# Input gates of a GRU quad in three chunks of 512 columns instead of four of 384

## The reference

```python
def cell(h, x):                       # 64 times, one after the other
    gi = x @ W_ih + b_ih              # [32, 512] @ [512, 1536]
    gh = h @ W_hh + b_hh
    r = sigmoid(i_r + h_r);  z = sigmoid(i_z + h_z)
    n = tanh(i_n + r * h_n)
    return (1.0 - z) * n + z * h
x = x + all_h                         # x: [32, 64, 512]
# blocks of 8 steps are summed, keys = blocks @ Wk.T with an RMS norm, softmax of keys . q
attended = einsum('bn,bnh->bh', attn, blocks)
y = x + attended @ Wo.T
x = x + layernorm(y) * ln_gamma + ln_beta
```

## Time and profile before

| what | us |
|---|---|
| median of 3 runs | 372.4 (371.16 to 372.96) |
| profiled execution, its own time | 371.04 |
| span from its first to its last instruction | 369.2 |
| TensorE busy | 361.8 (98%) |
| weight loads on record | 211.9 (57%) |
| VectorE busy | 264.3 (72%) |
| ScalarE busy | 167.5 (45%) |
| GpSimd busy | 11.9 (3%) |
| recurrent matmuls L628, 1920 records | 167.3 |
| input-gate matmuls L597, 720 records | 247.1 |

### The profile page before, as it was taken

How to read it: one execution, slowest core, us unless ns; L and a number is a source line. 1 busy time by engine, 2 the same in 40 slices (tenths; PEclk the granted TensorE clock), 3 DMA queues, 4 the chain that set the end, 5 groups by cost and what they waited for, 6 DMA issues and landing times.

```text
span 369.2 us, 9842 instructions
## 1 busy us (share of the span) xinstructions
PE 361.8 (98%) x3276; PEld 211.9 (57%) x3276; DVE 264.3 (72%) x1144; ACT 167.5 (45%) x525; POOL 11.9 (3%) x46
## 2 busy tenths in 40 slices
PE   8999999999999999999999999999999999999995
PEld 4456666555666555666555666555666655534762
DVE  2936767687676768776768767676868676888886
ACT  4834336262625343452626262434435255857430
POOL 6000000000000000000000000000000000000000
PEclk9999999999999999999999999999999999999999
DMA  7954635413232322324141323232232413110138
GB/s 308 419 157 102 193 93 167 110 36 100 74 99 71 99 71 58 91 64 107 44 105 42 99 71 99 71 99 70 51 99 57 113 38 77 52 30 28 33 136 320
DMA packets 27637, 38.37 MB, mean 104 GB/s; under 512 B 3033, under 2 KB 19033, under 8 KB 27617
## 3 DMA queue, kind: packets, MB, share of 16 engines
q1 hardware_dynamic: 27600, 38.09, 35.6%
q10 hardware_dynamic: 16, 0.02, 0.0%
HBM read 17.91 MB, written 4.19 MB: 60 GB/s over the span
## 4 chain that ended last, share of the span: by engine, by line
PE 90%; DVE 4%; issue 3%; DMA 1%; ACT 1%; DVEq 0%; POOLq 0%; SPq 0%; POOL 0%; ACTq 0%
PE gates_ps L628 43%; PE gi_ps L597 37%; PE gi_ps L610 1%; DVE gcx L1205 1%; PE first_ps L678 1%; PE fourth_ps L628 1%; PE third_ps L628 1%; PE keys_ps L628 1%; PE first_ps L628 1%; PE fourth_ps L678 1%; PE third_ps L678 1%; PE keys_ps L678 1%; DMA h_tok<-hist 1%; PE fourth_ps L666 1%; PE gates_ps L660 0%
## 5 line engine op out<-in xcount | busy, mean ns | idle before, releaser
L628 PE MATMUL gates_ps<-w_hh,turned 128*32 128x384 f32 x1920 | 167.3, 489 | 0.4 <-DVE turned L854 0.3
L628 PEld LDWEIGHTS gates_ps<-w_hh,turned 128*32 128x32 f32 x1920 | 56.4, 109 | 84.7 <-issue 55.5
L597 PE MATMUL gi_ps<-w_ih_hi,xt_hi 128*128 128x384 f32 x240 | 86.7, 363 | 0.0
L478 ACT ACTIVATE rz<-gates_ps 128x256 f32<-128x256 f32 x59 | 22.7, 385 | 128.5 <-PE gates_ps L628 128.5
L597 PE MATMUL gi_ps<-w_ih_hi,xt_lo 128*128 128x384 f32 x240 | 80.7, 338 | 0.0
L597 PE MATMUL gi_ps<-w_ih_lo,xt_hi 128*128 128x384 f32 x240 | 79.7, 334 | 0.0
L916 DVE TENSOR_TENSOR rz<-gates_ps,rz 128x128 f32<-128x128 f32 x59 | 17.2, 292 | 75.6 <-ACT rz L478 75.5
L597 PEld LDWEIGHTS gi_ps<-w_ih_hi,xt_hi 128*128 128x128 f32 x240 | 44.9, 187 | 37.5 <-issue 37.5
L597 PEld LDWEIGHTS gi_ps<-w_ih_lo,xt_hi 128*128 128x128 f32 x240 | 45.1, 188 | 0.0
L597 PEld LDWEIGHTS gi_ps<-w_ih_hi,xt_lo 128*128 128x128 f32 x240 | 44.9, 187 | 0.0
L854 DVE STREAM_TRANSPOSE turned<-hist 128x32 f32<-128x32 f32 x189 | 36.1, 216 | 2.1
(11 more groups left out here) (232 smaller groups left out, 297.1 us busy)
## 6 DMA issues: line engine op xcount, KB each, us to landing
gi<-gi_tok SPq DMA_DIRECT2D x60, 192.0 KB, 3.4
x1t<-in_x_t_dram SPq DMA_DIRECT2D x16, 256.0 KB, 3.2
gcx<-in_x_tok_dram SPq DMA_DIRECT2D x16, 256.0 KB, 3.2
h_tok<-hist SPq DMA_DIRECT2D x64, 64.0 KB, 2.2
out_dram<-gcx SPq DMA_DIRECT2D x16, 256.0 KB, 2.1
gcx<-in_w_ih_dram SPq DMA_DIRECT2D x4, 768.0 KB, 6.7
w_hh<-in_w_hh_dram SPq DMA_DIRECT2D x4, 768.0 KB, 9.0
wo_t<-in_wo_t_dram SPq DMA_DIRECT2D x1, 1024.0 KB, 5.7
```

The source lines that it names most:

```text
L478: act.activation(rz[:], gates_bank(t)[:, P:3 * P], ACT.Sigmoid).then_inc(rz_ready, 1)
L597: mm = pe.matmul(gi_ps[tok][:, 0:G3], a[:, k, :], w[:, k, gi_cols(j)], start=(m == 0), stop=(m == 3 * NJ - 1))
L628: mm = pe.matmul(gates_bank(t)[j * B:(j + 1) * B, P:], before[:, k * B:(k + 1) * B], chunk(w_hh, k, j), start=False, stop=(k == NJ - 1), s ...
```

## The change

The input gates of a quad are cut otherwise: 3 chunks of 512 columns (a whole PSUM bank) instead of 4 of 384. Chunk 0 is r and z of quarters 0 and 1, chunk 1 r and z of quarters 2 and 3, chunk 2 n of all four. The 36 matmuls are dealt out by nines: `gi_part` number 0 in the step tt = 3 of the quad two before it, parts 1 to 3 at tt = 0, 1, 2. So chunk 0 ends 3 matmuls into part 1, chunk 1 6 matmuls into part 2, chunk 2 at the end of part 3. keep_gi and move_gi run at tt = 0, 1, 2 and not at tt = 3. A chunk of r and z is moved by two DMAs (128 KB each, 1 KB pieces), that of n by four (64 KB each, 512 B pieces), so eight moves per quad, counted by one semaphore for each kind of chunk. ScalarE waits for the r and z moves alone before a quad's first seed, and VectorE waits for the n moves before n_pre in a quad's first step. Three bias quarters are copied before the scan and the fourth in step 0. gi_tok grows by 1 KB per partition, and small tiles of the end move to free columns of b_in.

The diff without the parts that only rename a tile or its brackets:

```diff
@@ -47,7 +47,7 @@
         xt_lo = sb("xt_lo", [P, NJ, P], F32R)
-        gi_tok = sb("gi_tok", [P, 2, G3])
+        gi_tok = sb("gi_tok", [P, 2, D])
         gi = sb("gi", [P, 2, Q * G3])
@@ -119,7 +119,7 @@
         x_t_in, x_tok_in, h_tok_in = sem("x_t_in"), sem("x_tok_in"), sem("h_tok_in")
-        gi_moved = [sem("gi_moved0"), sem("gi_moved1")]
+        gi_moved = [sem("gi_moved_rz0"), sem("gi_moved_rz1"), sem("gi_moved_n")]
         zeros_made, bias_cleared, own_made, made = sem("zeros_made"), sem("bias_cleared"), sem("own_made"), sem("made")
@@ -177,6 +177,19 @@
+        def chunk_cols(row, c):
+            by_quarter = row.rearrange("p (j c) -> p j c", j=NJ)
+            return by_quarter[:, :, 0:P] if c == 2 else by_quarter[:, 2 * c:2 * c + 2, P:G3]
+        def chunk_rows(tile, c):
+            return tile.rearrange("p (j c) -> p j c", j=(2, 2, NJ)[c])
+        def chunk_of(i, s):
+            return i * 6 + 3 * (s // Q) + s % Q
         def gates_bank(t):
@@ -212,15 +225,18 @@
-                idx, pos = i * S + s + 5, s + 5
-                q, j = i * 2 + pos // Q, pos % Q
-                slot, tok = (pos // Q) % 2, pos % 2
-                wait(sp, gi_tok_ready, idx + 1 - Q)
-                if j == 0 and not (isinstance(q, int) and q < 3):
+                q, c = i * 2 + s // Q + 1, s % Q
+                slot, tok = (s // Q + 1) % 2, chunk_of(0, s) % 2
+                wait(sp, gi_tok_ready, chunk_of(i, s) + 1)
+                if c == 0 and not (isinstance(q, int) and q < 3):
                     wait(sp, x1t_ready, q - 1)
-                sp.dma_start(gi[j * B:(j + 1) * B, slot, :], gi_tok[:, tok, :]).then_inc(gi_moved[tok], 16)
+                quarters = range(NJ) if c == 2 else (2 * c, 2 * c + 1)
+                for number, j in enumerate(quarters):
+                    rows = gi[j * B:(j + 1) * B, slot, :].rearrange("p (t c) -> p t c", t=Q)
+                    cols = slice(0, P) if c == 2 else slice(P, G3)
+                    sp.dma_start(rows[:, :, cols], chunk_rows(gi_tok[:, tok, :], c)[:, number]).then_inc(gi_moved[c], 16)
@@ -256,7 +272,7 @@
-                    if not (last and i * S + s + 5 >= T):
+                    if s % Q < Q - 1 and not (last and s >= Q):
                         move_gi(i, s)
@@ -292,7 +308,6 @@
             sp.dma_start(rms_tok, rows_d[None, 2 * D:].broadcast_to([P, D])).then_inc(consts_in, 16)
-            move_gi(0, -1)
             sp.wait_ge(w_lo_ready, NJ)
@@ -372,7 +387,7 @@
                 wait(act, x_t_in, quad * 16)
-                wait(act, gi_done, (quad - 1) * Q)
+                wait(act, gi_done, (quad - 1) * 3)
                 act.activation(xt_hi[:], x1t_of(quad), ACT.Copy).then_inc(x_hi_ready, 1)
@@ -393,7 +408,7 @@
             act.wait_ge(bias_kept, 1)
-            for j in range(2):
+            for j in range(NJ - 1):
                 keep_b_in(j)
@@ -405,8 +420,8 @@
-                    for tok in range(2):
-                        wait(act, gi_moved[tok], (i * 2 + s // Q) * 32)
+                    for c in range(2):
+                        wait(act, gi_moved[c], (i * 2 + s // Q) * 32)
                 first = (s % Q) * G3
@@ -487,8 +502,8 @@
                     seed_rz(i, s + 1, t + 1)
-                if peeled and s < 2:
-                    keep_b_in(s + 2)
+                if peeled and s == 0:
+                    keep_b_in(NJ - 1)
                 if s % Q == 2 and not last:
@@ -579,30 +594,35 @@
         def _(pe):
-            def gi_chunk(idx, pos, quad, lo_last=False):
-                tok, j = pos % 2, pos % Q
-                if j == 0:
+            def gi_part(quad, slot, number):
+                if number == 0:
                     wait(pe, x_lo_ready, quad)
-                wait(pe, gi_tok_ready, idx - 1 - Q)
                 terms = ((xt_hi, w_ih_hi), (xt_hi, w_ih_lo), (xt_lo, w_ih_hi))
-                order = [(k, a, w) for k in range(NJ) for a, w in terms]
-                if lo_last:
-                    order = [(k, a, w) for a, w in (terms[0], terms[2], terms[1]) for k in range(NJ)]
-                for m, (k, a, w) in enumerate(order):
+                for m in range(9 * number, 9 * number + 9):
+                    c, (k, term) = m // 12, divmod(m % 12, 3)
+                    lo_last = c == 0 and isinstance(quad, int) and quad == 1
+                    if lo_last:
+                        term, k = divmod(m % 12, NJ)
+                        term = (0, 2, 1)[term]
+                    tok = (slot * 3 + 3 + c) % 2
+                    a, w = terms[term]
+                    if m % 12 == 0:
+                        wait(pe, gi_tok_ready, quad * 3 - 3 + c - 1)
                     if lo_last and w is w_ih_lo:
                         pe.wait_ge(w_lo_ready, k + 1)
-                    mm = pe.matmul(gi_ps[tok][:, 0:G3], a[:, k, :], w[:, k, gi_cols(j)], start=(m == 0),
-                                   stop=(m == 3 * NJ - 1))
-                mm.then_inc(gi_done, 1)
+                    mm = pe.matmul(gi_ps[tok][:], a[:, k, :], chunk_cols(w[:, k, :], c), start=(m % 12 == 0),
+                                   stop=(m % 12 == 11))
+                    if m % 12 == 11:
+                        mm.then_inc(gi_done, 1)
...
-                    pe.wait_ge(gi_tok_ready, T - 1 - Q + group)
+                    pe.wait_ge(gi_tok_ready, 3 * (NQ - 1) - group)
                     pe.wait_ge(wk_in, 16)
@@ -628,8 +648,9 @@
                 mm.then_inc(gates_ready, 1)
-                if not (last and t + 5 >= T):
-                    gi_chunk(t + 5, s + 5, i * 2 + (s + 5) // Q)
+                if not (last and s >= Q - 1):
+                    q = (s + 1) // Q + 1
+                    gi_part(i * 2 + q, q % 2, (s + 1) % Q)
                 if last and 3 <= s < S - 1:
@@ -681,7 +702,7 @@
             pe.wait_ge(w_hi_ready, NJ)
-            gi_chunk(Q, Q, 1, lo_last=True)
+            gi_part(1, 1, 0)
             pe.wait_ge(made, 9 + 3 * NJ)
@@ -824,13 +845,13 @@
-            def keep_gi(idx, pos):
-                tok, j = pos % 2, pos % Q
-                wait(dve, gi_done, idx + 1 - Q)
-                wait(dve, gi_moved[tok], (idx - tok - Q) * 8)
-                dve.tensor_tensor(gi_tok[:, tok, :], gi_ps[tok][:, 0:G3], b_in[:, gi_cols(j)],
+            def keep_gi(i, s):
+                tok, c, q = chunk_of(0, s) % 2, s % Q, i * 2 + s // Q + 1
+                wait(dve, gi_done, chunk_of(i, s) + 1)
+                wait(dve, gi_moved[(1, 2, 0)[c]], ((q - 1) * 32, (q - 1) * 64, q * 32)[c])
+                dve.tensor_tensor(chunk_rows(gi_tok[:, tok, :], c), chunk_rows(gi_ps[tok][:], c), chunk_cols(b_in[:], c),
                                   ALU.add).then_inc(gi_tok_ready, 1)
@@ -917,6 +938,8 @@
                 wait(dve, rh_ready, t + 1)
+                if tt == 0 and bank is gates_ps:
+                    wait(dve, gi_moved[2], quad * 64)
                 for number, c in enumerate((first, rest)):
@@ -936,16 +959,13 @@
-                if peeled and s == 0:
-                    dve.wait_ge(b_in_ready, 1)
-                    keep_gi(Q, Q)
-                if peeled and s < Q - 1:
-                    dve.wait_ge(b_in_ready, s + 2)
+                if peeled and s < 2:
+                    dve.wait_ge(b_in_ready, (2, NJ)[s])
                 if tt == 0 and not (peeled and s < Q):
                     wait(dve, x1t_ready, quad)
-                if not (last and t + 5 >= T):
-                    keep_gi(t + 5, s + 5)
+                if tt < Q - 1 and not (last and s >= Q):
+                    keep_gi(i, s)
                 if tt == 2 and not last:
@@ -960,6 +980,7 @@
                 if last and s == 2:
+                    dve.wait_ge(gi_tok_ready, 3 * (NQ - 1))
                     dve.tensor_reduce(last_part, x1t[:, NQ - 1].rearrange("p k (b t) -> p (k b) t", t=Q), AX.X,
```

More of the change, by code:

```diff
@@ L62, in gru_block_attention @@
         tok_of_b = sb("tok_of_b", [P, P])
-        step_of_tok = sb("step_of_tok", [P, Q])
         own_n = sb("own_n", [P, NJ])
@@ L79, in gru_block_attention @@
         s2_tok = sb("s2_tok", [P, NQ])
-        s2_steps = sb("s2_steps", [P, NQ, Q])
-        s2 = sb("s2", [P, NQ])
+        late = b_in[:, 2 * D + P:2 * D + 2 * P]
+        s2_steps = late[:, 0:NQ * Q].rearrange("p (q t) -> p q t", t=Q)
+        s2, step_of_tok = late[:, 64:64 + NQ], late[:, 80:80 + Q]
         wo_sum = sb("wo_sum", [P, NJ])
         key_ss, key_dot = sb("key_ss", [P, 2]), sb("key_dot", [P, 2])
-        key_rms, score = sb("key_rms", [P, 2]), sb("score", [P, 2])
-        score_n = sb("score_n", [P, 2, NJ])
-        early = sb("early", [P, 32])
+        key_rms, score = late[:, 84:86], late[:, 86:88]
+        score_n = late[:, 88:96].rearrange("p (h n) -> p h n", n=NJ)
+        early = late[:, 100:128]
         odds, weights, rest_of = early[:, 0:4], early[:, 4:8], early[:, 8:12]
         early_odds, early_weights, early_rest = early[:, 12:16], early[:, 16:20], early[:, 20:24]
```

(14 more changed lines are left out.)

## The result

| | before | after |
|---|---|---|
| median of the runs, us | 371.83 (371.16 to 372.96, 4 runs) | 368.3 (368.13 to 368.6, 4 runs) |
| ratio of the times | | 0.9922, interval 0.9901 to 0.9943 |
| profiled execution: span, us | 369.2 | 366.3 |
| one step of the scan, us | 5.020 | 4.980 |
| gates part / input-gate part of a step, us | 2.72 / 2.30 | 2.72 / 2.26 |

The kernel became faster by 3.5 us, or 0.8%, which is more than the 0.5% that a measurement can tell. The forecast was 7.5 us: 364.9, with a range of 362.3 to 369.5, and 368.3 lies near its slow end.

A forecast was written before the change was run, and what follows sets the result against it. The prediction took TensorE to bound the scan at 5.02 us a step, the element-wise chain close behind. 59 steps x 0.135, plus 0.15, less 0.6, made 7.5 us: 364.9 us, range 362.3 to 369.5.

The forecast's parts named there:

- The seven gaps of 0.215: Input-gate part on TensorE: later starts of 512-column matmuls 0.215 us apart, giving a part of 2.14 to 2.15 against 2.30.
- The first gap: Input-gate part on TensorE: the first two of nine 512-column matmuls start 0.31 us apart, read from one f32r pair.
- the sum's first term: Scan steps: 59 steps, each 0.135 us shorter (step 4.885), 7.97 us in all.
- a load of 0.19: TensorE's stationary-operand load, 0.19 us, outlasts a 384-column stream of 0.160, the likely reason for gaps of 0.176.
- Rival (a): Input-gate gaps grow with columns, or nine matmuls meet the extra as often as twelve: gain 0 to 1.5 us; chance 0.11.
- rival (c): Chunk starts amid a part, or waits in the chain, cost their upper ends: gain 2.9 to 5 us; chance 0.15.
- chunk starts amid a part: TensorE's stream at matmuls 12 and 24 of 36: 0 to 0.1 us each, at most 3 us in all, taken as 0.
- The chain and its hand-over: Element-wise chain, transpose to gates: hand-over 0.15 us, floor about 4.88 a step, letting 0.135 of 0.155 through.
- The n wait: VectorE before n_pre in a quad's first step: 0 to 0.09 us, taken as 0.04, 0.6 us for 15 quads.
- VectorE's addition: Bias addition on VectorE at 512 columns: 0.69 us against 0.55, three times a quad, nothing on the path.
- strided operands: Input-gate matmuls with moving operands picked out in two runs of 256 or four of 128 columns: costed at nothing.
- rival (b): The four n moves run one after another, stalling 1.5 us in each of 15 quads: 15 us slower, 388; chance 0.06.

The follow-up runs named there:

- bench: Changed kernel with 13 streams of 12 matmuls behind the last real one, one property varied each; executed once; 512-column f32r gaps settle at 0.227 us.
- eight: Changed kernel with one of the nine input-gate matmuls of each part left out; 360.25 us, ratio 0.9717.
- eight_early: Changed kernel with eight matmuls a part and VectorE's n-part wait moved to the start of a quad's first step; 359.05 us, ratio 0.9703.
- contig: Changed kernel with the input gates' moving operand read as one run of 512 (wrong) columns; 368.26 us, ratio 0.9931.
- after_again: The changed kernel unchanged, run again as a yardstick beside the other runs; 368.16 us, ratio 0.9927.

## Why the prediction was right in sign and wrong in size

**The seven gaps of 0.215: the step that failed.** They measure 0.226 to 0.235, mean 0.230: 7 x 0.015 = 0.10 us a step. The first gap was 0.337 where 0.31 stood, 0.03 more; the last, 0.318, was right. (As written the three terms add up to 2.135; the prediction has 2.14 to 2.15.) So a part costs 2.26 and not 2.145, and TensorE's step became 0.04 us shorter, not 0.155. Of these 0.155 the forecast let the chain pass on 0.135; all of the 0.04 came through. So 5.6 us of the 8.0 in the sum's first term (59 x (4.980 - 4.885)) never came. Two readings failed. The 0.43 between the keys matmuls was halved, but those are f32 matmuls and pay 0.003 in both passes together; f32r pays 0.0134 each. And the f32r pair with its 0.31 was one first gap, from which a difference taken at 384 columns was subtracted; in the loop the first gap at 512 exceeds the later ones by 0.11, like 0.280 - 0.173 at 384, but it is itself 0.337. The prediction also explained the 0.176 by a load of 0.19 that outlasts the stream. bench refutes that: gaps of 0.112 at 128 columns with the same loads, and no gain at 512 from fewer stationary columns.

**Rival (a) was nearer, and not right either.** Its first half, a gap in proportion to the columns, would give 0.235 and nothing saved; its second, an extra that nine meet as often as twelve, the same. Measured is an extra per matmul, so 12 against 9 does count: 3 x 0.0134 = 0.040 us a step, 2.4 us in all. Before the change this could have been read from the chunk of the earlier trace rows, of which two more lines are

```profile
154.19 0.33 PE L597 MATMUL gi_ps<-w_ih_hi,xt_hi 128*128 128x384 f32 x1
...
154.88 0.33 PE L597 MATMUL gi_ps<-w_ih_lo,xt_hi 128*128 128x384 f32 x1
```

The mean of 0.176 mixes early gaps of up to 0.185 with late ones of (154.88 - 154.19) / 4 = 0.173. 384 columns at 2.4 GHz are 0.160, and the simplest carrying over to 512 is 0.213 + 0.013.

**The range held by luck.** 368.3 lies where rival (c) was to put it, 367.4 to 369.5, but what (c) charges for, chunk starts amid a part and waits in the chain, cost nothing on the path. The forecast by itself ended at 367.

**The chain and its hand-over: mis-sized, without effect.** 0.15 and the limit of 4.88 were taken from the tail; eight shows 0.055 in the loop and a floor of 4.80. The reason given for a smaller value in the loop, weights queued behind a working array, is not borne out: in eight's steps 4 to 7 and 56 to 59 the array works as in the loop, and the hand-over is 0.15. "turned" ahead of the gates did not become the bound: after, 0.23 us stay in hand in three steps of four and 0.135 in the first.

**The n wait.** 0.6 us were taken off for it. It costs 0.09 on VectorE where 0.04 was taken, in 12 quads and not 15, but nothing on the path, because the step stayed TensorE's. eight and eight_early show both halves of this.

**What held.** VectorE's addition (0.683 against 0.69), no price for strided operands (contig, bench), none for the chunk starts amid a part (parts with and without a chunk's start all take 2.26), the n moves hidden, rival (b) with its serial moves not seen (landings 2.1 to 3.6 us), no DMA wait ahead of the seed, the bias copies hidden. The 2.0 us that the prediction cites from the Trainium skill (DMA: Bandwidth & Descriptors, Anatomy of one DMA) stands there for DMAs that GpSimd issues; SyncE issues these.

**The count.** The span became 2.9 us shorter, and 59 x 0.040 = 2.4 of them are the steps. The rest is at the ends: the first gates matmul starts at 18.87 and not 19.78, but step 0 then takes 5.54 us, since it waits for w_hh, and what follows the last step's gates is 0.2 shorter. after_again shows the kernel without that difference: its first gates start at 19.84, as before, and its span is 366.7, which is 2.5 us less, 2.4 of them in the steps. Against the 7.5 us forecast, then: 5.6 less from the steps, 0.1 less from the first part, 0.6 more because the n wait wasn't paid, which makes 2.4. The medians moved by 2.6 us in after_again's comparison (370.79 to 368.16) and by 3.5 in the first; about 1 us of the 3.5 is start and spread, and was not traced further.

## What to carry to other kernels

Fewer, wider matmuls over the same columns save only the fixed part of each start, so read that part first: the late gaps of a stream in the timeline less columns / 2.4 GHz, from a stream of the same type as the one to be changed, never from another type or from a single pair, and not from a mean that mixes early gaps with late ones. Where a stream is the bound, the type of its operands can be worth more than its width, provided that equal types stand together. Before pricing what a second chain lets through, take its hand-over from the loop itself; the tail, like other steps written out around the loop, showed nearly three times as much. Where a range holds, ask by which of its terms.

## What the runs showed of the hardware

- At the 2.4 GHz level f32r matmuls follow each other at columns / 2.4 + 0.013 to 0.016 us (0.120, 0.147, 0.173, 0.202 and 0.227 at 256 to 512 columns) once a stream has settled; before that its 512-column gaps vary from 0.224 to 0.236. At 128 columns the gap is 0.112. bf16 has + 0.002, f32 + 0.003 for each two passes to 512 columns. Why f32r has the extra stays open.
- Behind the 128*32 matmuls of the gates the first 512-column gap is 0.337 for f32r and 0.226 for bf16.
- Behind a group of f32r the first bf16 matmul of 512 columns takes 0.227 and the next ones 0.216; f32r, bf16, bf16 in turn take as long as three f32r ones (0.680). Which unit waits there is open.
- Moving operands in two or four runs, a change of bank, start and stop flags all leave the 512-column gap at 0.227, and stationary operands of 32 or 64 columns at 0.224 to 0.236.
- A met semaphore wait placed in front of an instruction of VectorE's chain costs 0.09 us in the loop and, ahead of the same instruction, nothing in the written-out steps. Transpose to waiting TensorE is 0.055 in the loop and in steps 1 to 3, and 0.15 in steps 4 to 7 and in those written out behind the loop. Both are open.
- Moves within the SBUF land 2.2 us after issue at 64 KB, 3.0 at 128 KB and 3.4 at 192 KB (the kernel before); four issues by SyncE last 2.5 us. Those of h_tok stayed so (2.2 and 2.1) when the gi moves became eight a quad in place of four.
